# Who normalises the attention inputs: VectorE or GpSimd

## What is computed

```python
def _layernorm(x, axis=-1, eps=1e-05):
    m = jnp.mean(x, axis=axis, keepdims=True)
    v = jnp.var(x, axis=axis, keepdims=True)
    return (x - m) / jnp.sqrt(v + eps)

# reference, cut
x = x + L0_xattn(_layernorm(x), ctx, Wq, Wkv)    # 16 heads of 16, 120 context rows
x = x + L0_ffn(_layernorm(x), ...)               # shared part + top 2 of 8 experts
x = x + L1_xattn(_layernorm(x), ctx, ctx, mask, Wq, Wk, Wv)
x = x + L1_ffn(_layernorm(x), weight, bias)      # 6 bit block quantised linear
```

## Time and profile before

| | us |
|---|---|
| median of 3 runs | 1071.89 (1071.48 to 1074.15) |
| the profiled execution, its own time | 1070.92 |
| its span, first to last instruction | 1069.1 |
| attention phase | about 0 to 296 |
| routing | about 296 to 355 |
| experts | about 355 to 890 |
| second layer | about 890 to 1069 |

### The profile page before, as it was taken

The page is one execution under the profiler, slowest core; times in us unless marked ns, Lnnn a source line. Parts: engine busy times, 40 slices in busy tenths (PEclk is TensorE's granted clock), DMA queues, the critical chain, the costliest instruction groups (busy, mean ns, idle before and its releaser), DMA issues.

```text
span 1069.1 us, 21031 instructions
## 1 busy us (share of the span) xinstructions
PE 945.4 (88%) x7159; PEld 808.6 (76%) x7159; DVE 560.1 (52%) x1231; ACT 497.1 (46%) x1257; POOL 539.3 (50%) x654
## 2 busy tenths in 40 slices
PE   6999999999823699999999999999999989787776
PEld 4777777777612699999999999999999978554544
DVE  3888888888769223433223223322322313679882
ACT  3666666666642233333333333333333324666663
POOL 2333333333325455555565565555556532578883
PEclk9999999999955799999999999999999998999998
DMA  5434343433217521222221221222222244122201
GB/s 142 142 111 152 100 153 101 156 103 135 80 22 203 148 41 30 41 37 35 41 40 31 41 40 32 40 40 33 39 41 36 35 91 118 43 76 90 90 33 35
DMA packets 74709, 80.11 MB, mean 75 GB/s; under 512 B 12752, under 2 KB 69904, under 8 KB 74480
## 3 DMA queue, kind: packets, MB, share of 16 engines
q1 hardware_dynamic: 58704, 60.12, 18.6%
q0 software_dynamic: 15904, 18.66, 11.1%
HBM read 52.51 MB, written 26.25 MB: 74 GB/s over the span
## 4 chain that ended last, share of the span: by engine, by line
PE 60%; DVE 20%; issue 8%; POOL 6%; ACT 5%; DMA 2%; POOLq 0%; SPq 0%; DVEq 0%; ACTq 0%
PE b_H L1269 24%; PE b_Y L1281 23%; DVE a_max L635 5%; DVE a_probs L641 4%; PE a_T L506 2%; ACT a_probs L738 2%; PE a_S L496 2%; PE b_xT L1256 1%; PE c_g_ps L1940 1%; PE c_v_ps L1945 1%; POOL a_rstd L401 1%; PE c_f_ps L1911 1%; DVE a_xin L625 1%; ACT c_xn L1804 1%; DVE c_x L1773 1%
## 5 line engine op out<-in xcount | busy, mean ns | idle before, releaser
L1435 ACT ACTIVATE b_hiddenT<-b_H,b_b 128x128 f32<-128x128 f32 x568 | 162.4, 368 | 331.9 <-PE b_H L1269 331.9
L1269 PEld LDWEIGHTS b_H<-b_rowsT,b_w 128*128 128x128 f32 x2272 | 266.6, 193 | 6.0 <-ACT b_rowsT L1444 2.4
L1269 PE MATMUL b_H<-b_rowsT,b_w 128*128 128x128 f32 x2272 | 267.3, 276 | 1.8 <-ACT b_rowsT L1444 1.8
L1281 PE MATMUL b_Y<-w_sb,b_hiddenT 128*128 x1136 | 256.8, 379 | 0.0
L1227 POOL DMA_INDIRECT ffn_rows<-b_y,scatter_idx x71 | 154.0, 2169 | 193.7 <-DVE b_y L1360 185.2
L1281 PEld LDWEIGHTS b_Y<-w_sb,b_hiddenT 128*128 128x128 f32 x1136 | 210.5, 190 | 25.7
L1356 DVE TENSOR_TENSOR b_y<-b_Y,b_bc 128x256 f32<-128x256 f32 x71 | 30.2, 425 | 324.1 <-PE b_Y L1281 324.1
L1349 DVE COPY b_w<-w_sb 128x2048 f32 x71 | 87.1, 1227 | 37.5 <-issue 26.0
L635 DVE TENSOR_REDUCE a_max<-a_S 128x8 f32<-128x960 f32 x64 | 73.6, 1149 | 26.9 <-PE a_S L496 25.1
L1213 POOL DMA_INDIRECT b_rows<-xn_rows,gather_idx x71 | 73.5, 1035 | 21.5 <-issue 19.7
L744 ACT COPY a_probsT<-a_T 120x512 f32<-120x512 f32 x128 | 69.1, 594 | 28.1 <-PE a_T L506 28.1
(11 more groups left out here) (219 smaller groups left out, 1367.2 us busy)
## 6 DMA issues: line engine op xcount, KB each, us to landing
w_sb<-in_L_ffn_W SPq DMA_DIRECT2D x32, 512.0 KB, 4.5
a_xin<-in_x SPq DMA_DIRECT2D x16, 256.0 KB, 3.0
a_xres<-in_x SPq DMA_DIRECT2D x32, 128.0 KB, 2.0
xn_rows<-a_xn SPq DMA_DIRECT2D x32, 128.0 KB, 2.3
x_rows<-a_x SPq DMA_DIRECT2D x32, 128.0 KB, 2.0
ffn_rows<-shared SPq DMA_DIRECT2D x2, 2048.0 KB, 18.6
c_x<-x_rows SPq DMA_DIRECT2D x16, 256.0 KB, 2.7
c_acc<-ffn_rows SPq DMA_DIRECT2D x16, 256.0 KB, 2.7
```

What stands on the lines that cost most here:

```text
L1269: j = pe.matmul(H_ps[i][:, c * P:(c + 1) * P], w1c[i][:, k * HID + c * P:k * HID + (c + 1) * P], xT[:, k * P:(k + 1) * P], start=(k == 0), ...
L1281: j = pe.matmul(y_ps[i][:, 0:D], hT[i][:, c * P:(c + 1) * P], w2_sb[:, bass.ds(e * (HB * D) + c * D, D)], start=(c == 0), stop=(c == HB - 1))
L1435: j = act.activation(hT[i][:, c * P:(c + 1) * P], H_ps[i][:, c * P:(c + 1) * P], ACT.Gelu, bias=b1c[i][:, c:c + 1])
```

## The change

The function `normalise1` moves from VectorE's program to GpSimd's. Its two instructions stay what they were, tensor_scalar with a subtraction and a multiplication and two operands of one number per partition. GpSimd issues them right behind `inverse_std1` of the same batch, in all 16 places; the wait on `s_r1` moves with them, and `s_xn` is raised by GpSimd. Nothing else changes.

```diff
--- before.py
+++ after.py
@@ -400,6 +400,13 @@
                 ge(pool, s_xn, b)
                 pool.tensor_tensor(rstd1[:], ve1[:], half[:], ALU.pow).then_inc(s_r1, 1)
 
+            def normalise1(b):
+                pool.wait_ge(s_r1, 2 * b + 2)
+                for v in range(2):
+                    i = pool.tensor_scalar(xn[:, v, :], xin[:, v, :], mv1[:, v, 0:1],
+                                           rstd1[:, v:v + 1], ALU.subtract, ALU.mult)
+                i.then_inc(s_xn, 1)
+
             def inverse_std2(t):
                 pool.wait_ge(s_st2, 2 * t + 2)
                 pool.tensor_scalar(ve2[:], mv2[:, 1:2], EPS, None, ALU.add).then_inc(s_r2, 1)
@@ -428,8 +435,10 @@
                 i.then_inc(s_kbd, 1)
 
             inverse_std1(0)
+            normalise1(0)
             key_blocks(0)
             inverse_std1(1)
+            normalise1(1)
             pool.wait_ge(s_bet, 16)
             for t in range(TILES):
                 b, u = t // 2, t % 2
@@ -442,6 +451,7 @@
                     inverse_std2(t - 1)
                 if u == 1 and batch(b + 2):
                     inverse_std1(b + 2)
+                    normalise1(b + 2)
             add_beta(TILES - 2)
             residual(TILES - 1)
             inverse_std2(TILES - 1)
@@ -619,13 +629,6 @@
                     i = dve.bn_aggr(mv1[:, v, :], bn1[:, v, :])
                 i.then_inc(s_st1, 1)
 
-            def normalise1(b):
-                dve.wait_ge(s_r1, 2 * b + 2)
-                for v in range(2):
-                    i = dve.tensor_scalar(xn[:, v, :], xin[:, v, :], mv1[:, v, 0:1],
-                                          rstd1[:, v:v + 1], ALU.subtract, ALU.mult)
-                i.then_inc(s_xn, 1)
-
             def scores_of(h):
                 return S_ps[:, :, h * PAIR:(h + 1) * PAIR].rearrange("p r (j c) -> p r j c",
                                                                      c=CTX)
@@ -673,10 +676,8 @@
                 dve.tensor_copy(logits[:, t * E:(t + 1) * E], M_ps[:, D:SG]).then_inc(s_sg, 1)
 
             stats1(0)
-            normalise1(0)
             dve.wait_ge(s_xnT_p, 1)
             stats1(1)
-            normalise1(1)
             dve.wait_ge(s_sbb, 16)
             for t in range(TILES):
                 b, u = t // 2, t % 2
@@ -694,8 +695,6 @@
                     keep_shared(t - 2)
                 if tile(t - 1):
                     normalise2(t - 1)
-                if u == 1 and batch(b + 2):
-                    normalise1(b + 2)
             t = TILES - 1
             over_sums(t)
             stats2(t)
```

## The result

| | before | after |
|---|---|---|
| median of 6 runs, us | 1072.97 | 1078.66 |
| ratio to before, 95% interval | | 1.0068 [1.0053, 1.0083] |
| the profiled execution's span, us | 1069.1 | 1076.5 |
| first `largest` starts at | 15.92 | 17.30 |
| from there to VectorE's last copy of logits | 289.46 | 295.25 |

The forecast was 4.5 us faster; the kernel is 5.7 us slower by the medians and 7.4 by the two spans. The spans split into 1.4 us at the start, 5.8 from there to the last logits and 0.2 behind that. Of the 5.8, 14 batches at 0.41 explain 5.7. What is left nearly cancels: the first batch took some 0.9 us more than the change accounts for (17.85, against 16.90 in the kernel with 192 columns further down, which has the same gain there), and the stretch from the last `largest` to the last logits took 0.9 less (14.58 against 15.50).

The account below looks back on a forecast made before the run. It took the attention stage's chain of waits, 17.5 us a batch, as the bound, not one engine. Terms: -4.7 in the loop, +0.2 at the start, -4.5 in all, 1071.89 to 1067.4 us; range 1065.5 to 1072.5.

Parts of the forecast that it names:

- the price of the added instruction: Moved `normalise1` on GpSimd: 0.44 us an instruction, from the 128x2 tensor_scalar's 230 ns and a cast's slope per column.
- The bound that I kept for the range at 729 ns: Near upper end for one moved GpSimd instruction: two-tensor `residual` of the same size, 729 ns, still free on the path.
- the far end, 1.23: Farther upper price of one moved GpSimd instruction: one two-tensor pass for each of its two operations, 1.23 us.
- Rival (3): GpSimd takes a pass per operation, 1.23 us; `turn_inputs` late, +7.4 in the loop, +1.7 at the start, about 1081; chance 0.10.
- a pair of 1.5 us: Moved pair on GpSimd by the skill page's 2x: about 1.5 us, still inside 1.60, sum unchanged.
- The gain, 0.33 at 14 boundaries: Odd-to-even tile boundaries in the loop: without `normalise1` on VectorE, `largest` starts 0.33 us earlier (first 0.40), 4.7 us in all.
- 28 us of VectorE's time: Attention phase: 17.3 us in `normalise1` plus 10.9 idle ahead of it for GpSimd's power; most of it not to be had.
- It moves up with the path: Rest of each batch behind `largest`: waits on TensorE and ScalarE leave room, so the full 0.33 us counts per batch.
- The room of 1.60: GpSimd's pair at the boundary may take 1.60 us, 0.80 an instruction, before late `turn_inputs` costs time; slip allowed 0.26.
- The start: Batch 0, normalised ahead of the loop with nothing hiding it: `turn_inputs` +0.2 us later, between 0 and 0.8.
- The collision: VectorE's pair takes 1.14 us beside `add_beta` against 0.73 at the start: 0.41 is contention, already in the 0.33.
- `largest` pays nothing: VectorE's `largest` beside GpSimd's moved pair: no contention added; paying 0.41 again would make the sum +1 us.

Follow-up runs that it names:

- the kernel with 192 columns: The changed kernel, but GpSimd's two instructions normalise only the first 192 of 256 columns; one run, 1.01 us an instruction, period 17.53 us.
- Half the columns: The changed kernel, but GpSimd's two instructions normalise only the first 128 of 256 columns; ratio to before 0.9965, period 17.24 us.
- a row tile each: The kernel before, but in the loop VectorE normalises the first row tile of a batch and GpSimd the second; ratio to before 0.9960, period 17.24 us.

## Why the prediction was wrong, point by point

**The step that failed** is the price of the added instruction: "That gives 230 + 254 x 0.83 = 440 ns", and "I take 0.44, since the instruction reads one tensor as the cast does, and per-partition numbers are read once". It measured 1.229 us, with all 32 instances between 1.218 and 1.239, and the gain that the added time was to leave alone became a loss. The price of a column was 3.3 ns and not 0.83: I took the slope from another kind of instruction. That is 0.63 us of the 0.79 missing; the rest is the fixed part, 0.38 by the two lengths measured against 0.23. No run shows how often per-partition numbers are read; two of them in place of immediates cost 0.14 us (1.22 against 1.08). The rows had no tensor_scalar with more than two columns, so they could not give one. The bound that I kept for the range at 729 ns was no bound either; only the far end, 1.23, held.

**The far end was right by luck.** Rival (3) priced a pass of tensor_tensor for each operation, 1.23 us. The size is that of the measurement, the mechanism isn't: one operation costs 0.88 to 0.93 and the second adds 0.2 to 0.3. I gave it 0.10, though no row spoke against it.

**The skill's rule.** The page "GPSIMD Engine Reference" (4.1, Engine selection) of the Trainium skill speaks of about 2x on two inputs and roughly line rate on one; I took its 2x to a pair of 1.5 us. The pair measured 2.45 us against VectorE's 0.73, 3.3 times, though the instruction reads one tensor. The measurement decides: the rule's direction held, the size of neither part did.

**The gain, 0.33 at 14 boundaries**: right. `largest` starts 0.07 behind the scores in every kernel that moves, splits or clears the way for the pair, and four of them reach a period of 17.23 to 17.24, 0.3 under before. That 28 us of VectorE's time stood against 4.7 that could be won was right as well.

**It moves up with the path**: right, including ScalarE's copies, which were 0.02 us from being the later path. Half the columns shows it: 0.30 of the 0.33 arrives in the period.

**The room of 1.60**: right in kind, 0.14 too small. I had limited it by `keys` (0.26) ahead of `turn_xn2`; in the changed kernel `turn_xn2` starts while the end of `keys`, as the trace models it, still lies ahead. What limits it is `turn_back` and the reciprocal, for which I had 0.31. In the changed kernel they follow `turn_inputs` by 1.13 us in all, so it may start 2.25 - 1.13 = 1.12 behind `largest`; I had allowed 0.96. At 1.23 an instruction I had +0.53 a batch; it was +0.41.

**The start**: the rival's +1.7 was +1.4 in the trace (up to 2.05 against other starts of the same form), my +0.2 wrong with the price.

**The collision**: "0.41 us of it is contention" was in the prediction, and was the better idea in it: 1.14 us becomes 0.74 where `add_beta` waits. The page "SBUF — State Buffer" (Who interferes with whom) of the Trainium skill tells of an exclusive lock on which the later of the two waits for the whole of the other's instruction. That the later one pays agrees with the rows: 1.23 becomes 1.37 on GpSimd where it starts second, 0.40 becomes 0.66 on VectorE where it does, and the earlier one takes its usual time. That it waits for the whole instruction does not: `normalise2` ended 0.54 us before the GpSimd instruction that had started ahead of it. The measurement decides. That `largest` pays nothing was right, but not by the row that I gave for it: `add_beta` had ended at 155.65 when `largest` started at 156.04. The changed kernel shows it: `largest` runs wholly beside GpSimd's pair and takes 1.16, as at the odd boundary.

## What to carry to other kernels

Price an instruction that moves to GpSimd by its own form: if the trace has no row of that kind and length, the range must hold the far bound and the chance must say that nothing is known, since a slope borrowed from another instruction was wrong by a factor of four here. Before work is moved off an engine, see whether it is slow there because of a neighbour: a wait that moved the neighbour behind it gave all of the gain. And where the new place is slow, work out by when its result is wanted, not only how long it takes: with the same 2.4 us on GpSimd a batch got 0.4 us longer or 0.3 shorter, by when they began.

## What the runs showed of the hardware

GpSimd's tensor_scalar on 256 columns costs more than its tensor_tensor, even where the latter gets its second operand from one column, broadcast: 0.93 against 0.61 us for one operation with the same operands. Two of the latter in a row, an estimated 1.22 by these rows, would cost as much as the one with two operations.

TensorE's granted clock fell for some microseconds between 19 and 28 us in some executions and not in others. The window from 20 to 30 us of the kernel before, and of the one with a row tile each (busy us and instructions by engine, granted clock, DMA):

```profile
20.00:30.00 10.00, 8.81 (x101) 6.38 (x99) 6.06 (x9) 6.93 (x12) 1.86 (x3) 1.00 0.17 41
```

```profile
20.00:30.00 10.00, 9.40 (x72) 6.83 (x73) 3.70 (x5) 4.55 (x8) 1.75 (x3) 0.66 0.07 21
```

The first batch took 19.66 us there and 17.30 in the kernel before. 0.66 is the mean of a stretch with both levels: taken by the microsecond, the clock is 0.50 (1.2 GHz) from 21 to 27 us and 1.00 (2.4 GHz) from 28 on. TensorE was as busy in the ten microseconds ahead in both (6.8 and 6.9 us of 10), and the two programs issue the same instructions up to there. Of the nine executions, one of each kernel, three show this at 0.66 to 0.69, three at 0.83 (the changed kernel's among them), and three not at all; what sets it off stays open. The end of the attention phase, from the last `largest` to the last logits, took 14.5 to 14.6 us where the mean granted clock over it was 0.87 or 0.88, 15.5 at 0.76 or 0.77, and 15.8 and 16.0 at 0.75 and 0.73. That is why the periods are compared from the second batch on. The ratios of the four kernels with equal periods, 0.9960 to 0.9972, lie within each other's intervals.
